# Layer 0 of a four-layer graph network: the counting chain of the next group cut into pieces, and the A/C product moved between the halves of a graph's first chunk

## The reference

```python
mask = (adj > 0.0)                                # [B, N, N], about 12% ones
xj_proj = x @ W1a                                 # H = 192
h = relu(xj_proj[:, :, None] + (x[:, :, None] - x[:, None]) @ W1b + b1)
hm = einsum('bjkh,bjk->bjh', h, mask)             # sum over the neighbours k of j
return hm @ W2 + deg[..., None] * b2
```

## Time and profile before

| | |
|---|---|
| median of 3 runs | 1564.76 us (1564.12 to 1565.76) |
| the profiled execution's own time | 1565.16 us |
| its span | 1563.5 us (1.66 us less than its own time) |
| PE, DVE, ACT, POOL busy | 1388.9, 1165.4, 1104.2, 493.9 us |
| layer 0 in the trace | about 50 to 1092 us |

### The profile page before, as it was taken

The page is one execution under the profiler, slowest core; times in us unless marked ns, Lnnn a source line. Parts: engine busy times, 40 slices in busy tenths (PEclk is TensorE's granted clock), DMA queues, the critical chain, the costliest instruction groups (busy, mean ns, idle before and its releaser), DMA issues. The chain is left out here.

```text
span 1563.5 us, 41736 instructions
## 1 busy us (share of the span) xinstructions
PE 1388.9 (89%) x11307; PEld 1063.7 (68%) x11308; DVE 1165.4 (75%) x3087; ACT 1104.2 (71%) x2424; POOL 493.9 (32%) x610
## 2 busy tenths in 40 slices
PE   0799999999999999999999999998899997972398
PEld 0477777777777777777776777766788887920398
DVE  6688888888888888888888888887344444978655
ACT  0788788787887878878788787875455554916675
POOL 0233333333333333333333333333111111056300
PEclk9999999999999999999999999999899998976699
DMA  6000000000000000000000000000000000000022
GB/s 142 15 9 8 15 7 7 7 7 13 7 7 7 10 10 7 7 7 11 9 7 7 7 13 7 0 1 2 1 0 0 0 0 0 0 1 0 6 49 54
DMA packets 40750, 18.08 MB, mean 12 GB/s; under 512 B 19397, under 2 KB 40711, under 8 KB 40711
## 3 DMA queue, kind: packets, MB, share of 16 engines
q1 hardware_dynamic: 40178, 17.39, 4.5%
q10 hardware_dynamic: 532, 0.21, 0.1%
HBM read 13.40 MB, written 4.19 MB: 11 GB/s over the span
## 5 line engine op out<-in xcount | busy, mean ns | idle before, releaser
L807 DVE SCALAR_TENSOR_TENSOR acc<-slot_banks,acc 128x768 f32<-128x768 f32 x512 | 487.4, 952 | 98.7 <-PE slot_banks L551 85.3
L869 POOL TENSOR_TENSOR acc<-acc 128x384 f32<-128x384 f32 x128 | 127.7, 998 | 642.0 <-DVE onediff L801 628.1
L551 PE MATMUL slot_banks<-ac_hi,work 128*128 128x192 f16 x1408 | 256.1, 246 | 4.6 <-ACT slot_banks L714 1.4
L551 PE MATMUL slot_banks<-ac_lo,work 128*128 128x192 f16 x1408 | 255.8, 246 | 0.0
L551 PE MATMUL slot_banks<-ac_hi,onediff 128*128 128x192 f16 x1024 | 191.0, 247 | 22.8 <-DVE acc L807 16.2
L551 PE MATMUL slot_banks<-ac_lo,onediff 128*128 128x192 f16 x1024 | 189.5, 246 | 0.0
L551 PEld LDWEIGHTS slot_banks<-ac_hi,work 128*128 (+1 forms) x1408 | 137.3, 98 | 30.9 <-issue 11.9
L789 DVE TENSOR_SCALAR work<-work,slot_key 128x1024 f16 x256 | 121.3, 480 | 30.5 <-issue 30.5
L551 PEld LDWEIGHTS slot_banks<-ac_lo,work 128*128 (+1 forms) x1408 | 137.8, 98 | 8.4 <-issue 0.2
L551 PEld LDWEIGHTS slot_banks<-ac_hi,onediff 128*128 x1024 | 102.1, 100 | 56.1 <-issue 51.2
L707 ACT ACTIVATE work<-slot_banks 128x576 f32<-128x576 f32 x128 | 82.7, 646 | 73.9 <-PE slot_banks L551 72.7
(11 more groups left out here) (252 smaller groups left out, 3326.9 us busy)
## 6 DMA issues: line engine op xcount, KB each, us to landing
adj_in<-in_adj_dram SPq DMA_DIRECT2D x32, 256.0 KB, 2.8
out_dram<-acc SPq DMA_DIRECT2D x32, 128.0 KB, 2.0
l1w<-in_L_gnn_W_dram SPq DMA_DIRECT2D x2, 64.0 KB
l1b<-in_L_gnn_b_dram SPq DMA_DIRECT2D x2, 64.0 KB
x_all<-in_x_dram SPq DMA_DIRECT2D x4, 0.2 KB, 11.9
nm_in<-in_nodemask_dram ACTq DMA_DIRECT2D x1, 64.0 KB
w1a<-in_L_gnn_W_dram ACTq DMA_DIRECT2D x1, 48.0 KB
w1b<-in_L_gnn_W_dram ACTq DMA_DIRECT2D x1, 48.0 KB
```

The lines of the kernel that those rows point to most:

```text
L551: last = nc.tensor.matmul(unit(pair, t, 1), hot(t), part[:, q, H:2 * H].unsqueeze(1), start=False, stop=(e == 1 and (t % SB == SB - 1 or t ...
L807: nc.vector.scalar_tensor_tensor(out=sums, in0=unit((q + k) % 2, 0, SU), scalar=0.0, in1=sums, op0=ALU.min, op1=ALU.add).then_inc(s_free[k ...
L869: nc.gpsimd.tensor_tensor(acc[:, q, 0:2 * H], acc[:, q, 0:2 * H], acc[:, q, 2 * H:4 * H], ALU.add)
```

## The change

`pe_ac` of graph b+2 moves from a step's start to between half 0 and half 1 of its first chunk (`first_done`). On DVE `dve_counts` is cut into five functions that are called in five places of step q = 1; the first part of `dve_first_rows` moves into step q = 2, between two halves; the first part of `dve_host_rows` moves ahead of the statistics of graph b-3. On ACT, at q = 0, the shared slots' ranks go ahead of the AC copies, and the next group's mask ahead of the pads. No arithmetic is added or removed. The core of the diff:

```diff
             pe_half(pe, 0, q, at, cnt, True)
+            first_done()
             if not (known(b) and b == 0):
                 pe.wait_ge(s_seed, b)
...
                 def step(b, g, u, q, nxt, p, use):
-                    if not (known(b) and b + 2 >= B):
-                        pe_ac(pe, b + 2, *group_of(b, g, u, q, -2))
+                    def first_done():
+                        if not (known(b) and b + 2 >= B):
+                            pe_ac(pe, b + 2, *group_of(b, g, u, q, -2))
...
+                    if q == 0 and not (known(g) and g == 0):
+                        act_host_slots(act, g, u)
                     if not (known(b) and b + 2 >= B):
                         act_ac(act, b + 2, (q + 2) % GS)
-                    if q == 0 and not (known(g) and g == 0):
-                        act_host_slots(act, g, u)
+                    if nxt is not None and q == 0:
+                        act_adj(act, nxt, p)
                     if not (known(b) and b + 1 >= B):
                         act_pads(act, b + 1, *group_of(b, g, u, q, -1))
                     if nxt is not None:
-                        if q == 0:
-                            act_adj(act, nxt, p)
...
                     def halfway():
                         if not (known(b) and b < 2):
                             dve_update(dve, b - 2)
+                        if nxt is not None and q == 1:
+                            dve_full(dve, nxt)
+                        if nxt is not None and q == 3:
+                            dve_past_last(dve, nxt)
+                        if not (known(b) and b < 2):
+                            dve_updated_stats(dve, b - 2)
                         if nxt is not None and q == 3:
                             dve_host_rows(dve, nxt, p)
+
+                    def middle():
+                        if nxt is not None and q == 1:
+                            dve_count_full(dve, nxt)
+                        if nxt is not None and q == 2:
+                            dve_first_rows(dve, nxt, p)
+
+                    def beside():
+                        if nxt is not None and q == 1:
+                            dve_own(dve, nxt)
+
+                    def summed():
+                        if nxt is not None and q == 1:
+                            dve_left(dve, nxt)
 
                     def late():
                         if nxt is not None:
                             if q == 0:
                                 dve_rows(dve, nxt)
                             if q == 1:
-                                if not (known(b) and b < 2):
-                                    dve.wait_ge(s_W2, b - 1)
-                                dve_counts(dve, nxt, p)
+                                dve_pieces(dve, nxt, p)
                             if q == 2:
-                                dve.wait_ge(s_W2, b - 1)
-                                dve_first_rows(dve, nxt, p)
+                                dve_from_first(dve, nxt, p)
```

More of the change, by code:

```diff
@@ L569, in pe_next_half, with pe_slots @@
                 .then_inc(s_done[k], 1)
-        def pe_slots(pe, b, g, u, q, regs, halfway, between):
+        def pe_slots(pe, b, g, u, q, regs, first_done, halfway, between):
             cnt, prev, pos, later = regs
@@ L745, in dve_counts, with dve_count_full, dve_own @@
              .then_inc(s_nop, 1)
+        def dve_count_full(dve, g):
+            v = nc.vector
             dve.wait_ge(s_nop, 12 * g + 5)
             v.tensor_reduce(nfull[:, :], over[:, :, :], AX.X, ALU.add).then_inc(s_nop, 1)
+        def dve_own(dve, g):
+            v = nc.vector
             dve.wait_ge(s_nop, 12 * g + 6)
@@ L751, in dve_counts, with dve_left, dve_pieces @@
             v.tensor_scalar(own[:, :], nfull[:, :], float(SC), float(SC * MINC), ALU.mult, ALU.add).then_inc(s_nop, 1)
+        def dve_left(dve, g):
+            v = nc.vector
             dve.wait_ge(s_nop, 12 * g + 7)
             v.tensor_tensor(left[:, :], degp[:, :], own[:, :], ALU.subtract).then_inc(s_nop, 1)
+        def dve_pieces(dve, g, p):
+            v = nc.vector
             dve.wait_ge(s_nop, 12 * g + 8)
@@ L775, in dve_first_rows, with dve_past_last @@
                 nc.vector.tensor_scalar(host[:, p, q * N:(q + 1) * N], row16[:, :], start[:, q:q + 1], None, ALU.is_ge)
-        def dve_host_rows(dve, g, p):
+        def dve_past_last(dve, g):
             for q in range(GS):
@@ L781, in dve_host_rows @@
             last.then_inc(s_nop, 1)
+        def dve_host_rows(dve, g, p):
             dve.wait_ge(s_nop, 12 * g + 12)
@@ L808, in dve_half, with dve_slots @@
                                            op0=ALU.min, op1=ALU.add).then_inc(s_free[k], 1)
-        def dve_slots(dve, b, g, u, q, regs, halfway, late):
+        def dve_slots(dve, b, g, u, q, regs, halfway, middle, beside, summed, late):
             cnt, prev, pos, old, count_reg = regs
@@ L831, in dve_slots @@
             dve_half(0, q)
+            middle()
             dve_shared_onehot(dve, g, u, q)
+            beside()
             dve.wait_ge(s_done[1], cnt)
@@ L835, in dve_slots @@
             dve_half(1, q)
+            summed()
             if not (known(b) and b == B - 1):
@@ L932, in between @@
                                 pe_host_ranks(pe, nxt, p)
-                    pe_slots(pe, b, g, u, q, regs, halfway, between)
+                    pe_slots(pe, b, g, u, q, regs, first_done, halfway, between)
                 all_iterations(pe, step)
@@ L994, in _ @@
                 dve_rows(dve, 0)
-                dve_counts(dve, 0, 0)
+                dve_full(dve, 0)
+                dve_count_full(dve, 0)
+                dve_own(dve, 0)
+                dve_left(dve, 0)
+                dve_pieces(dve, 0, 0)
                 dve_first_rows(dve, 0, 0)
+                dve_from_first(dve, 0, 0)
+                dve_past_last(dve, 0)
                 dve_host_rows(dve, 0, 0)
@@ L1014, in late @@
                             if q == 1:
-                                if not (known(b) and b < 2):
-                                    dve.wait_ge(s_W2, b - 1)
-                                dve_counts(dve, nxt, p)
+                                dve_pieces(dve, nxt, p)
                             if q == 2:
-                                dve.wait_ge(s_W2, b - 1)
-                                dve_first_rows(dve, nxt, p)
-                    dve_slots(dve, b, g, u, q, regs, halfway, late)
+                                dve_from_first(dve, nxt, p)
+                    dve_slots(dve, b, g, u, q, regs, halfway, middle, beside, summed, late)
                 all_iterations(dve, step, prefetch_back_edge=True)
@@ L1026, in _ @@
                     dve_update(dve, b)
+                    dve_updated_stats(dve, b)
                 dve.wait_ge(s_x0, B)
```

4 lines of the change are left out of this document (3 added, 1 removed).

## The result

The changed kernel takes 1524.78 us (median of 4, 1521.91 to 1525.92) against 1565.26 us for the kernel before on the same chip: ratio 0.9737, 95% interval 0.9721 to 0.9752, so 40 us less; 1529 was forecast. The profiled execution took 1521.91 us, its span 1520.2 us. Layer 0 carries it: the first seeds of steps 4 and 124 stand at 87.06 and 1022.33 us, a group takes (1022.33 - 87.06) / 30 = 31.18 us instead of 32.52, and 1.34 times 30 is 40 us.

The account below looks back on a forecast made before the run. No engine is full; PE sets the pace with short waits for engines that wait for PE in turn. Terms sum to -1.24 us a group, rounded to -1.2, times 30 groups: -36 us, forecast 1529 us, range 1508 to 1548.

Parts of the forecast that it names:

- 2.5 us of waits: PE's short waits for other engines in a group of four steps, about 2.5 us, the most that reordering can give.
- AC between the halves: First chunk: DVE starts its first half earlier, so PE's waits of 0.22 us (q = 0) and 0.18 (q = 1) vanish.
- the register load stays hidden: PE's step start: load early in all four steps, so exposures of 0.30 us (q = 2) and 0.28 (q = 3) vanish.
- the danger: PE's step start: without AC's cover, 0.95 us of load and register steps stand exposed; as a rival 1604 us, chance 0.10.
- The counting chain: DVE, end of q = 1: 1.06 us taken off the path and 0.38 added among large operations, saving 0.68.
- The rival of small operations at full price: DVE's moved operations keep their full price: path saves 0.38 us instead of 0.68, 1541 us; chance 0.18.
- the third case: DVE's moved small operations each keep their 0.2 us, by the skill's rule; listed as a rival at 1541 us, chance 0.18.
- The wait left at q = 2: PE's wait for DVE at the second chunk's half 0 falls from 0.66 us to 0.46.
- ACT's order at q = 0: Pads go behind the mask, which comes about 0.8 us earlier, so PE's wait of 0.26 us for it vanishes.
- q = 3 gives some back: PE's wait for ACT's seed before half 1 grows from 0.31 us to 0.59; the step gets 0.20 longer.
- The sum: Per group: -0.48 us at q = 0, -0.48 at q = 1, -0.48 at q = 2, +0.20 at q = 3, together -1.24.

Follow-up runs that it names:

- act_only: The kernel before with only ACT's order at q = 0 changed; 1559.1 us, ratio 0.9952.
- ac_late: The changed kernel with the AC product behind half 1 instead of between the halves; 1665.4 us, ratio 1.0634.
- load_held: The changed kernel with one wait added ahead of PE's register load, for ACT's copy of the transposed sums; 1553.6 us, ratio 0.9913.
- no_ac: The changed kernel with the AC product at the step's start again; 1549.6 us, ratio 0.9897.
- ac_only: The kernel before with only the AC product moved, DVE's and ACT's orders as before; 1582.1 us, ratio 1.0095.
- no_chain: The changed kernel with DVE's order of before, the counting functions whole and where they were; 1543.2 us, ratio 0.9855.

## Why the prediction was right, step by step

- **What bounds the kernel, and 2.5 us of waits.** Right in kind, too small in size. Steps q = 0 and q = 1 lost 0.73 and 0.70 us, where the waits that I counted are 0.48 each. Most of the missing 0.25 and 0.22 is at the exit of PE's loop: behind a second chunk that had waited for DVE, the transposes start 0.24 us after the last gather, in the changed kernel 0.08. At q = 0 another 0.07 is the mask, which was worth 0.33 and not 0.26 (act_only); the rest, 0.02 and 0.06, I can't place. PE's timeline of the changed kernel at q = 1, and that of the kernel before at the same place:

```profile
566.08 0.25 PE L551 MATMUL slot_banks<-ac_lo,onediff 128*128 128x192 f16 x1
566.16 0.38 PE L522 MATMUL bank<-ident,acc 128*128 128x128 f32 x2
```

```profile
620.71 0.25 PE L551 MATMUL slot_banks<-ac_lo,onediff 128*128 128x192 f16 x1
620.95 0.43 PE L522 MATMUL bank<-ident,acc 128*128 128x128 f32 x2
```

  A wait inside the loop goes with 0.16 us more at its exit. This holds at q = 0, 1 and 2 of all fourteen kernels (0.24 to 0.25 in the median where the second chunk waited, 0.08 or 0.09 where it didn't), apart from q = 0 of ac_late with its lower clock. That the queue, held at the wait, then does the exit in the open is my reading and not shown: at q = 3 of the changed kernel the exit takes 0.21 though no gather of the second chunk is late. This is the term that I left out.
- **AC between the halves; the register load stays hidden.** Right: the seeds follow at 0.08, the load is 0.9 to 1.6 us ahead in the middle groups, and with ACT's new order the AC copies' delay was swallowed. Only at q = 0 of every other group the seeds come 0.19 late. Load and register steps take 0.97 by the rows, not 0.95; before, they were exposed by 0.31 and 0.29 us at the start of q = 2 and q = 3 in the median, where I had 0.30 and 0.28. load_held shows that the danger was real, no_ac that the move is worth 25 us with the others. What I didn't say is that alone it loses 16 us (ac_only).
- **The counting chain.** 0.68 us was forecast, 0.66 measured (no_chain). The rival of small operations at full price is out: 0.12 for the reduction, 0.15 for two together and 0.07 for `left`. (The prediction calls this rival the third case; it stands second in its list.) As to the Trainium skill's sentence that a semaphore between chained operations costs nothing extra (VectorE: DVE Perf Modes, "The DRAIN you can't avoid"), the trace doesn't bear it out for operations of 4 to 56 columns: some 0.2 us from one to the next where each waits for the one before, 0.07 to 0.15 among operations that don't.
- **The wait left at q = 2.** Mis-sized: 0.46 forecast, 0.65 to 0.70 measured. DVE got as much faster as forecast, but PE arrives there 0.16 us earlier by the loop's exit too.
- **ACT's order at q = 0.** Right, and under-rated: 0.33 us alone for 0.26, and 1.2 us a group (36 us) once the AC copies come later.
- **q = 3 gives some back.** Right: the wait for the seed is 0.58 (0.59 forecast), the step 0.18 us longer (0.20). Over all groups it is 0.26, by the late seeds of every other q = 0.
- **The sum.** -1.24 forecast, -1.34 measured. The errors are 0.25 and 0.21 at q = 0 and 1, and 0.21 and 0.06 the other way at q = 2 and 3: -1.43 in a steady group. Step 121, which nothing in the sum stands for, takes 0.09 of it back. So that 1529 lies 4 us from 1524.8 is in part luck: the mechanism was right, but errors of 0.2 us a group in both directions and one odd step mostly cancel. In the two profiles, the time from step 124 on, which the forecast left as it was, is 2.5 us shorter (497.9 against 500.4).

## What to carry to other kernels

Engines that wait for each other in turn hide the worth of a single edit: here the parts sum to -0.24 us a group one by one and to -1.34 together, and one of them alone is a loss. Kernels with two of the three parts tell which pair makes the difference. Judge an edit by the wait that ends last behind it, and try it together with the edits that make room for it. Before moving work away from a place, ask what it covered there (a register load, another engine's copy) and what stands ahead of that in the queue. Short dependent operations belong between long ones, but look at what the neighbouring engine runs at that moment.

## What the hardware showed that I had not expected

- A DVE operation on fp16 SBUF data waited for the end of the POOL operation under way: 0.9 us instead of 0.24 for the first of four (1.39 for the four), and 0.74 for all four once POOL was idle. In every kernel, wherever that first one takes longer than its 0.24 us, it ends 0.05 us behind POOL's operation. Not every DVE operation does this: BATCH_NORM_STATS2 on `x_all` takes 0.22 us beside POOL and without it, and a half (L829) 0.96 and 0.95.
- Behind a gap of some 2 us in PE's work, once every four steps, the granted clock of 22 steps in 30 was 0.74 to 0.85 of full, with matmuls 0.16 us apart for part of them; of the 100 us that ac_late loses, nearly 60 go with this clock.
- Behind a wait inside PE's hardware loop the loop's exit took 0.16 us longer than without one (0.24 against 0.08), but it took 0.21 at q = 3 with no late gather in the loop.
